# Self-attention of two feed-forward stages: scores issued last in a step, causal mask on TensorE, zero rows and first operand stacks loaded another way

## The reference

```python
scores = jnp.einsum('bqhd,bkhd->bhqk', q, k) / jnp.sqrt(jnp.float32(8))
scores = jnp.where(causal, scores, -jnp.inf)      # L2_ffn only
attn = jax.nn.softmax(scores, axis=-1)
out = jnp.einsum('bhqk,bkhd->bqhd', attn, v).reshape(B, S, 128) @ wo
```

## Time and profile before

| | |
|---|---|
| median of 3 runs | 2894.82 us (2891.86 to 2895.26) |
| the profiled execution, its own time | 2894.68 us |
| its span in the profile | 2893.0 us |
| mean granted clock of TensorE, share of full speed | 0.856 |
| PE busy | 2167.4 us (75%) |
| DVE busy | 1718.5 us (59%) |
| ACT busy | 1162.0 us (40%) |
| POOL busy | 664.8 us (23%) |
| first call, from its first instruction to its last exponential | 833.9 to 1144 us |
| second call, the same | 1971.2 to 2258 us |

### The profile page before, as it was taken

How to read it: one execution, slowest core, us unless ns; L and a number is a source line. 1 busy time by engine, 2 the same in 40 slices (tenths; PEclk the granted TensorE clock), 3 DMA queues, 4 the chain that set the end, 5 groups by cost and what they waited for, 6 DMA issues and landing times. The chain is left out here.

```text
span 2893.0 us, 36794 instructions
## 1 busy us (share of the span) xinstructions
PE 2167.4 (75%) x11488; PEld 1283.5 (44%) x11488; DVE 1718.5 (59%) x4410; ACT 1162.0 (40%) x2237; POOL 664.8 (23%) x711
## 2 busy tenths in 40 slices
PE   6774795766737887798789989673778697678397
PEld 4562572224622222565445444461223365567254
DVE  3676437997947774544555554344776345456677
ACT  2442336543424554222676766331434322133122
POOL 0430003543420000000565556331222000153000
PEclk7786796897958999799999999785899798688699
DMA  1000000001022210000333222102220001000000
GB/s 34 34 1 6 0 0 5 0 0 48 1 56 55 42 32 0 1 0 25 97 79 83 73 76 54 45 1 46 48 52 7 1 0 61 25 1 1 0 1 14
DMA packets 37759, 79.99 MB, mean 28 GB/s; under 512 B 6912, under 2 KB 21248, under 8 KB 36448
## 3 DMA queue, kind: packets, MB, share of 16 engines
q1 hardware_dynamic: 37344, 77.36, 10.4%
q10 hardware_dynamic: 256, 0.68, 0.1%
HBM read 51.80 MB, written 7.34 MB: 20 GB/s over the span
## 5 line engine op out<-in xcount | busy, mean ns | idle before, releaser
L659 ACT ACTIVATE spt<-P 128x1024 f32<-128x1024 f32 (+3 forms) x256 | 220.9, 863 | 291.9 <-PE P L509 291.6
L2127 PE MATMUL P<-XT,W 128*128 x424 | 220.8, 617 | 63.1 <-ACTq L2161 63.1
L2203 DVE SCALAR_TENSOR_TENSOR X<-P,WE,X 128x128 f32 x576 | 162.3, 344 | 166.8 <-PE P L2144 162.2
L2144 PEld LDWEIGHTS P<-W,e_h 128*128 128x128 f32 (+1 forms) x1952 | 220.4, 191 | 61.3 <-issue 57.1
L2144 PE MATMUL P<-W,e_h 128*128 128x128 f32 (+1 forms) x1952 | 227.5, 278 | 3.4 <-DVE X L2203 3.4
L963 POOL TENSOR_TENSOR d_e<-d_e,d_rc 128x512 f32<-128x512 f32 (+3 forms) x256 | 179.6, 723 | 176.8 <-DVE d_rc L870 144.1
L524 PE MATMUL P<-spt,sva 128*32 128x512 f32 (+3 forms) x1024 | 213.5, 542 | 0.2 <-POOL spt L697 0.2
L2172 ACT ACTIVATE e_g<-P 128x512 f32<-128x512 f32 x148 | 88.4, 597 | 309.8 <-PE P L2127 309.8
L608 DVE TENSOR_REDUCE smf<-P 128x2 f32<-128x1024 f32 x128 | 153.0, 1221 | 77.1 <-PE P L497 75.1
L911 ACT ACTIVATE d_e<-d_e,d_mn 128x512 f32<-128x512 f32 (+3 forms) x256 | 141.7, 554 | 132.7 <-DVE d_mn L862 132.3
L2190 DVE TENSOR_TENSOR e_h<-e_g,P 128x512 f32<-128x512 f32 x148 | 101.7, 687 | 109.7 <-PE P L2130 107.4
(11 more groups left out here) (336 smaller groups left out, 4384.1 us busy)
## 6 DMA issues: line engine op xcount, KB each, us to landing
d_bt<-in_alibi SPq DMA_DIRECT2D x32, 512.0 KB, 3.7
d_moved<-d_raw SPq DMA_DIRECT2D x256, 64.0 KB, 2.4
ska<-parts_k SPq DMA_DIRECT2D x96, 64.0 KB
sqa<-parts_q SPq DMA_DIRECT2D x96, 64.0 KB
W<-in_w_L_xattn SPq DMA_DIRECT2D x1, 4291.0 KB, 13.7
W<-in_w_L_ffn SPq DMA_DIRECT2D x1, 3333.0 KB, 11.9
W<-in_w_L_ffn SPq DMA_DIRECT2D x1, 3155.0 KB, 10.5
parts_k<-sparts SPq DMA_DIRECT2D x8, 384.0 KB, 2.3
```

The lines of the kernel that those rows point to most:

```text
L659: a.activation(PT[:, n % 2, :, t, N - late(t):N], P[:, BANK_T:BANK_T + 2, 0:late(t)], ACT.Exp, scale=SC).then_inc(s("exp"), 1)
L2127: pe.matmul(P[:, PG + j % 2, :], w["w1"][:, col:col + 128], x, start=True, stop=True).then_inc(s("gate"), 1)
L2144: last = pe.matmul(P[:, PY + j % 2, 128 * t:128 * (t + 1)], HT[rows, u % 2, blk, 128 * t:128 * (t + 1)], w2, start=n == 0, stop=n == len(p ...
L2203: last = v.scalar_tensor_tensor(x, y, k.WE[:, bass.ds(c * 4 + t, 1), e], x, ALU.mult, ALU.add)
```

## The change

In both calls:

- PE's step order becomes T, other, V (odd steps), S; DVE's becomes other, maximum. S is thus issued last in its step.
- Zero rows of the query stacks of batches 0 and 1 are sent first of all; later ones ahead of the k stack.
- The parts and the stack of q of batch 0 are issued from ACT's queue, while k's stay on SP's. The fill of the key stacks moves from POOL to ACT (one before the q DMAs, one after the copy of v). The weights of the next stage are loaded after batch 1's k parts are written.

In the causal call:

- The mask is added in PSUM by TensorE: after the two matmuls of S, two more (identity as weights, a 128x128 bfloat16 mask as moving operand) onto the last 128 columns of each head. The maximum is then one `tensor_reduce` of both heads, as in the other call.

```diff
+        def blank_rows(eng, b):
+            eng.wait_ge(s("zero"), 1)
+            for j in range(2):
+                eng.dma_start(QA[64 * j + ROWS:64 * j + 64, b % 2], ZERO[0:64 - ROWS, :].unsqueeze(1).to_broadcast([64 - ROWS, PAIRS, N])).then_inc(
+                    s(f"stack_q{b % 2}"), 16)
...
+            blank_rows(sp, 0)
+            blank_rows(sp, 1)
+            out_parts(sp, "k", 0)
+            sp.wait_ge(s("keys_ready"), 1)
+            stacked(sp, "k", 0)
+            for b in range(1, B):
+                out_parts(sp, "k", b)
+                if b == 1:
                     load_weights(k, i + 1)
+                    sp.wait_ge(s("keys_ready"), 2)
+                else:
+                    sp.wait_ge(s("score_t"), QT * PAIRS * (b - 1))
+                    blank_rows(sp, b)
+                stacked(sp, "k", b)
+                out_parts(sp, "q", b)
+                stacked(sp, "q", b)
...
                     last = pe.matmul(P[:, BANK_S + 2 * (c % 2) + h, 0:wide(u)], QA[r, b % 2, p, 128 * u:128 * (u + 1)], KA[r, b % 2, p, 0:wide(u)],
-                                     start=True, stop=True)
+                                     start=True, stop=not causal)
+                if causal:
+                    if c == 0:
+                        pe.wait_ge(s("mask"), 1)
+                    for h in range(2):
+                        last = pe.matmul(P[:, BANK_S + 2 * (c % 2) + h, wide(u) - 128:wide(u)], k.identb[:], MASK[:], start=False, stop=True)
                 last.then_inc(s("score"), 1)
...
                 for u in range(QT):
-                    if n < ITEMS:
-                        scores(n, u)
                     if 0 <= n - 2 < ITEMS:
                         transposed(n - 2, u)
                     for what, which in step_uses(n, u):
                         other(what, which)
                     if u % 2 == 1 and 0 <= n - 3 < ITEMS:
                         values(n - 3, (u - 1, u))
+                    if n < ITEMS:
+                        scores(n, u)
...
-                if not causal:
-                    v.tensor_reduce(MF[:, n % 2, u, :], P[:, bank:bank + 2, :], AX.X, ALU.max, negate=True).then_inc(s("max"), 1)
-                    return
-                if c >= 2:
-                    v.wait_ge(s("max"), c - 1)
-                for h in range(2):
-                    last = v.tensor_tensor_reduce(SPENT[:, c % 2, h, 0:wide(u)], P[:, bank + h, 0:wide(u)], MASK[:, N - wide(u):N], -1.0, 3e38,
-                                                  ALU.add, ALU.min, MF[:, n % 2, u, h:h + 1])
-                last.then_inc(s("max"), 1)
+                v.tensor_reduce(MF[:, n % 2, u, :], P[:, bank:bank + 2, 0:wide(u)], AX.X, ALU.max, negate=True).then_inc(s("max"), 1)
...
                 for u in range(QT):
-                    if n < ITEMS:
-                        maxima(n, u)
                     for what, which in step_uses(n, u):
                         if what not in on_a:
                             other(what, which)
+                    if n < ITEMS:
+                        maxima(n, u)
...
             a.activation(k.warm[:], k.ones[0:1, 0:1], ACT.Exp)
+            a.activation(KA[:, 0], k.max_rows.unsqueeze(2).to_broadcast([128, PAIRS, N]), ACT.Copy).then_inc(s("keys_ready"), 1)
+            out_parts(a, "q", 0)
+            stacked(a, "q", 0)
             other("v", 0)
+            a.activation(KA[:, 1], k.max_rows.unsqueeze(2).to_broadcast([128, PAIRS, N]), ACT.Copy).then_inc(s("keys_ready"), 1)
...
             g.memset(ZERO[:], 0.0).then_inc(s("zero"), 1)
+            g.memset(MB[:], 0.0).then_inc(s("blank"), 1)
             for n in range(2):
-                g.tensor_copy(KA[:, n], k.max_rows.unsqueeze(2).to_broadcast([128, PAIRS, N])).then_inc(s("keys_ready"), 1)
-                if n == 0:
-                    g.memset(MB[:], 0.0).then_inc(s("blank"), 1)
```

More of the change, by code:

```diff
@@ L378, in self_attention @@
         ZERO = sb("zero", N, dt=BF16)
-        MASK, SPENT = (sb("mask", N), sb("spent", 2, 2, N)) if causal else (None, None)
+        MASK = sb("mask", 128, dt=BF16)
         scratch = {x: nc.dram_tensor(f"parts_{x}_{k.serial}", (B * 128, 3 * N), BF16, kind="Internal").ap() for x in "qk"}
@@ L419, in step_uses, with out_parts @@
             return [(what, which) for m, part, what, which in order if m == n and part == u]
+        def out_parts(eng, x, b):
+            eng.wait_ge(s("cut_" + x), b + 1)
+            eng.dma_start(scratch[x][128 * b:128 * (b + 1), :], PARTS_OF[:, "kq".index(x)].rearrange("p c n -> p (c n)")).then_inc(s("written_" + x), 16)
+        def blank_rows(eng, b):
[3 more added lines that the diff above has]
+                    s(f"stack_q{b % 2}"), 16)
@@ L421, in _, with stacked @@
+        def stacked(eng, x, b):
+            y = "kq".index(x)
+            eng.wait_ge(s("written_" + x), 16 * (b + 1))
+            src = scratch[x][128 * b:128 * (b + 1), :].rearrange("(p j d) (c n) -> j c d p n", p=PAIRS, j=2, c=3)
+            for j in range(2):
+                for c, pair in enumerate(PARTS):
+                    eng.dma_start((KA, QA)[y][64 * j + 8 * c:64 * j + 8 * c + 8, b % 2], src[j, pair[1 - y]]).then_inc(s(f"stack_{x}{b % 2}"), 16)
         @block.sync
         def _(sp):
[L423 to L441, removed]
-                    load_weights(k, i + 1)
@@ L552, in _ @@
             if causal:
-                v.memset(MASK[:, 0:N - 128], 0.0)
-                step(v.tensor_copy(MASK[:, N - 128:N], k.cst[:, 128:256]))
+                v.tensor_copy(MASK[:], k.cst[:, 128:256]).then_inc(s("mask"), 1)
             def cut(x, b):
```

## The result

The change makes the kernel slower: 2922.68 us (median of 4 runs, 2918.13 to 2927.01) against 2893.34 (4 runs, 2884.72 to 2895.26), a ratio of 1.0107 with a 95% interval of 1.0081 to 1.0133. The forecast was 2914.1 and slower; between the profiled executions it said +19.4 us, and the spans differ by 32.3 (2893.0 and 2925.3).

A forecast was written before the change was run, and what follows sets the result against it. No engine is full; a ring of PE and ACT was seen in the timeline. Terms -18.7 - 2.4 + 5.4 + 5.7 + 22.2 + 7.2 = +19.4 on 2894.7 gave 2914.1 us, whole range 2875 to 2932.

The forecast's parts named there:

- The wait behind scores last: Call without mask: V waits 0.2 us for the placed maxima in 27 items, +5.4 us.
- Behind the cuts without mask: Six items with a cut of k or q: DVE's maxima come late, PE waits 1.15 us, +5.7 in all.
- Terms one and two: Call without mask: V's wait for the placed maxima, +5.4 us, and the longer wait behind cuts, +5.7.
- rival C: Slower still: waits behind the cuts let PE's clock fall, twelve cuts at about 1 us, 2926 us; chance 0.13.
- With mask: Causal call: scores last and mask matmuls lengthen items by 0.97 or 0.51 us, +22.2; six cuts add +7.2.
- the 0.23 us a step: Causal call, PE: price of the two mask matmuls in a step, between 0.107 and 0.46 us.
- The starts: Start of both calls: first S 7.7 and 11.0 us earlier, -18.7, and first T earlier, -2.4.
- the term of -2.4 for the first T: Start of each call: first T no longer behind an S awaiting a maximum, one reduce of 1.2 us earlier.
- the write's 3 us: Start of the calls: estimate for q's write among the stack DMAs plus the landing, 3 us.
- Rival A: Faster: scores last ends S's 27.0 us of waiting for DVE with mask, placed maxima in time, 2864.4 us; chance 0.20.
- Rival B: No change: the two DMA queues add up (-30.4) and the mask costs only its columns, 2893.1 us; chance 0.18.
- the ring: Loop of PE and ACT: V, S, even T, its exponential, odd T, V; claimed to get no shorter.

The follow-up runs named there:

- the order alone: Kernel before with only the scores issued last in a step on PE and DVE, mask and start as before: 2926.48 us, 1.0103 of before.
- doubled mask: Kernel before with the causal mask added by TensorE and each mask matmul issued twice; no other change: 2912.17 us in one run.

## Why the prediction was right, and where it was short

**The wait behind scores last: right.** Forecast 0.2 us an item without mask from 2.23 against 2.05; measured a chain of 2.25 and plain items 8.30 for 8.11. V moved ahead of the job takes the loop back to 263.1 (from 276.3), so that wait is the cause and not S's new place; with mask 0.06 to 0.10 us an item remain.

**Behind the cuts without mask: the wait was right, the clock was not in it.** Forecast 1.15 us for each, 0.2 of it from the term before; the step behind a cut of q went from 2.71 to 3.83, +1.12. Behind two of the three cuts of k the item grew by 2.76, as the clock fell after a wait of 1.06 us. Terms one and two gave +11.1 for the loop; it measured +14.0 with two such falls of 1.65 us, and +11.7 in the order alone with one. This is rival C, true in part: I gave the clock as a case of its own, where some of it belonged into the main sum for the k cuts. That the wait brings the fall about is likely but not shown, since the same wait also passed without it.

**With mask: right but for the mask's price.** The term that was mis-sized is the 0.23 us a step. From S of 256 columns to T it is 0.43 us after (2100.27 to 2100.70) and 0.12 with the order alone: 0.31. In items with a group job the mask stands at three uncovered places of the sum, so 0.08 more at each makes 0.97 into 1.21; 1.36 was measured (5.91 to 7.27), and 0.63 for 0.51 in the others (6.32 to 6.95). Items behind cuts grew by about 2.0, where 1.2 and the 0.97 of an item with a group job made 2.2. In all +31.9 for +29.4, a difference smaller than the loop's variation, while the plain items' is not.

The 0.23 was set beside a rule of the Trainium skill (TensorE: Matmul & The Clock Gate, "The mechanism" of packing small matmuls), by which a full-array load is not hidden. The doubled mask speaks against that reading: the second pair costs its columns alone, and its loads begin in the trace while the matmul ahead still runs, so they were hidden. The same section also lets a load into the background buffer go ahead, which I had left out. What is left over the columns, 0.2 us, stands at the two changes between half-array heads and the full array, and that section gives no figure for it; the runs do not part a load that waits there from any other cost of the change.

**The starts: right in size for S, too much in all.** First S 9.0 and 7.7 us nearer to the call's start, where 7.7 and 11.0 were forecast; first exponential 10.5 and 6.7 nearer, 17.2 for a forecast of 21.1. Of the 3.9 us between them, 1.9 are the term of -2.4 for the first T: from first S to first exponential it was 13.6 us in both calls and is 12.1 and 14.6, so -0.5 in all. The other 2.0 are the first S, and the missing step there is in the second call: I took the write's 3 us for both, but there it was issued behind k's stack and took 7.3. Kernels with an unchanged start show 33.3, 41.2, 36.2 and 37.1 us to the first S in call 1, so a difference of a few us there cannot be read from single runs, and 9.0 for a forecast of 7.7 is luck in part: the six other runs with the new start show 24.1 to 29.5 us where this one shows 24.3. In call 2 the unchanged ones lie within 39.3 to 41.5. The share of 0.58 with two stacks under way bears out that a second stack adds its own 7.6 us, as the earlier trace rows's rate has it. The Trainium skill (DMA: Bandwidth & Descriptors, "Issuing engines are not separate DMA queues") says that a second engine saves issue time only; with the write behind k's stack that agrees (34.0 us with one queue, 32.4 to 35.8 with two), and where it let the write go ahead, it saved 3.6 us of the write's own time besides.

**Rival A** had its premise right and its gain wrong. S's wait for DVE did shrink from 27.0 to 6.9 us. Little of it was a loss to begin with: the order alone halved it, to 13.4 us, and cost 19.2 us in that loop, as the wait for the placed maxima went from 12.0 to 26.8. **Rival B** fell with the share of 0.58 and the mask's 0.31. The change did what it says.

The sum fell 10 to 13 us short of what was measured (29.3 between the medians, 32.3 between the spans): 2.9 on the k cuts, 2.5 with mask, 3.9 on the starts, 3.6 outside the calls, where runs differ by as much.

## What to carry to other kernels

An instruction that stands behind a wait it has no part in pays for that wait: when producers move later in a loop, look for the job that consumes the last of them and move what does not need it (here V) ahead of the job. Put added work where the engine waits anyway: the same mask matmuls cost 0.97 us an item in the ring and 0.40 where most of them lay under an exponential. A second queue is worth most where it lets a small transfer start ahead of the large ones, not where it adds a stream to engines that are already shared.

## What the runs showed of the hardware

- A pair of full-array matmuls of 128 columns between two half-array ones cost 0.31 us on TensorE, with the same pair doubled 0.11 more.
- Two waits of PE, 0.91 and 1.06 us with few matmuls between them, were followed in the changed kernel two times of two by a granted clock of 0.50 (1.2 GHz) and a V of 3.4 us instead of 1.91. With the order alone they were followed once by 0.50 (3.15 us) and once by 1.00 (1.91 us).
- A write of 384 KB took 2.3 to 2.6 us in seven runs when issued ahead of the other queue's twelve stack DMAs. Behind them it took 6.6 to 8.9 us on a queue of its own, and 4.3 to 7.5 us on theirs.
- The conversion on DVE took 1.76 us beside a memset on POOL, and 5.51 beside a cast and a memset; both times it ended 0.3 us after POOL's last of them (838.39 and 846.40 us).
